# An explicit weight load ahead of two waits in each step of a recurrence on TensorE

## What is computed

```python
x = x + L0(x, cond)          # adaptive low-rank MLP over 4 x 512 rows of 256
x = x + L1(x, cond)          # a recurrence over the 512 time steps:
xW = jnp.einsum('ntd,dh->nth', x, Wx) + b
def step(prev_h, xw_t):
    next_h = jnp.tanh(xw_t + prev_h @ Wh)     # prev_h is 4 x 256, Wh is 256 x 256
    return (next_h, next_h)
```

## Time and profile before

| | us |
|---|---|
| median of 3 runs | 568.93 |
| lowest, highest run | 568.4, 570.08 |
| the profiled execution, its time | 569.51 |
| the profiled execution, its span from first to last instruction | 567.6 |
| of this, from the first tanh of the recurrence (80.49) to the last pair (562.66) | 482.2 |
| TensorE busy with matmuls / with weight loads | 510.9 / 429.1 |
| VectorE / ScalarE busy | 287.8 / 173.9 |

### The profile page before, as it was taken

The page is one execution under the profiler, slowest core; times in us unless marked ns, Lnnn a source line. Parts: engine busy times, 40 slices in busy tenths (PEclk is TensorE's granted clock), DMA queues, the critical chain, the costliest instruction groups (busy, mean ns, idle before and its releaser), DMA issues.

```text
span 567.6 us, 31977 instructions
## 1 busy us (share of the span) xinstructions
PE 510.9 (90%) x14200; PEld 429.1 (76%) x14200; DVE 287.8 (51%) x2214; ACT 173.9 (31%) x1128; POOL 21.6 (4%) x33
## 2 busy tenths in 40 slices
PE   4979989999999999999999999999999999999995
PEld 4334458888888888888888888888888888888884
DVE  2142355555555555555555555555555555555553
ACT  3021113333333333333333333333333333333322
POOL 1039100000000000000000000000000000000000
PEclk9978989999999999999999999999999999999999
DMA  7950000000000000000000000000000000000000
GB/s 259 387 190 0 0 3 4 4 13 5 13 4 13 4 14 4 13 5 10 8 3 14 3 14 3 14 3 14 3 14 3 13 5 14 3 11 6 6 13 12
DMA packets 11216, 15.99 MB, mean 28 GB/s; under 512 B 1587, under 2 KB 6978, under 8 KB 11074
## 3 DMA queue, kind: packets, MB, share of 16 engines
q1 hardware_dynamic: 11078, 13.95, 7.4%
HBM read 11.85 MB, written 2.10 MB: 25 GB/s over the span
## 4 chain that ended last, share of the span: by engine, by line
PE 82%; ACT 8%; issue 3%; SPq 3%; DMA 3%; DVE 0%; DVEq 0%
PE bank L653 66%; ACT w_sb L358 8%; PE bank L633 7%; PE bank L589 3%; DMA w_sb<-in_L_cond_W 3%; PE bank L601 2%; SPq L227 2%; PE bank L642 1%; PE bank L628 1%; PE bank L571 1%; PE bank L578 1%; PE bank L515 0%; PE bank L554 0%; ACT xT L315 0%; DVE x2T L446 0%
## 5 line engine op out<-in xcount | busy, mean ns | idle before, releaser
L653 PE MATMUL bank<-w_sb,whp 128*128 128x52 bf16 x6132 | 244.2, 186 | 38.7 <-ACT w_sb L358 38.0
L653 PEld LDWEIGHTS bank<-w_sb,whp 128*128 128x128 bf16 x6132 | 188.5, 96 | 86.8 <-ACT w_sb L358 64.5
L479 DVE TENSOR_TENSOR r_ring<-w_sb 128x4 f32<-128x4 f32 x1022 | 136.6, 164 | 220.9 <-ACT w_sb L358 218.5
L358 ACT ACTIVATE w_sb<-bank 128x4 f32<-128x4 f32 x1024 | 142.2, 174 | 324.7 <-PE bank L653 324.7
L653 PE MATMUL bank<-r_ring,whp 128*128 128x52 bf16 x4096 | 220.7, 186 | 0.0
L653 PEld LDWEIGHTS bank<-r_ring,whp 128*128 128x128 bf16 x4096 | 174.7, 96 | 0.0
L653 PE MATMUL bank<-l_ring,whp 128*128 128x52 bf16 (+1 forms) x2048 | 157.5, 178 | 0.0
L484 DVE TENSOR_TENSOR l_ring<-r_ring 128x4 bf16<-128x4 f32 x1024 | 135.9, 162 | 0.0
L653 PEld LDWEIGHTS bank<-l_ring,whp 128*128 128x128 bf16 x2048 | 122.3, 96 | 0.0
L633 PE MATMUL bank<-xp,wxp 128*128 128x32 bf16 x1536 | 76.2, 176 | 0.0
L633 PEld LDWEIGHTS bank<-xp,wxp 128*128 128x128 bf16 x1536 | 56.2, 95 | 0.0
(11 more groups left out here) (84 smaller groups left out, 147.6 us busy)
## 6 DMA issues: line engine op xcount, KB each, us to landing
w_sb<-in_L_cond_W SPq DMA_DIRECT2D x8, 1024.0 KB, 14.0
x_sb<-in_x SPq DMA_DIRECT2D x4, 512.0 KB, 9.6
out<-o_sb SPq DMA_DIRECT2D x64, 32.0 KB, 1.6
w_sb<-in_L_cond_W SPq DMA_DIRECT2D x1, 256.0 KB
up_sb<-in_L_cond_base_up SPq DMA_DIRECT2D x1, 256.0 KB, 3.1
down_sb<-in_L_cond_base_down SPq DMA_DIRECT2D x1, 256.0 KB, 11.1
wh_sb<-in_L_cond_Wh SPq DMA_DIRECT2D x1, 256.0 KB
wx_sb<-in_L_cond_Wx SPq DMA_DIRECT2D x1, 256.0 KB
```

The lines of the kernel that those rows point to most:

```text
L358: nc.scalar.activation(h_ring[:, m, slot(pair, s), 0:B], zt, ACT.Tanh).then_inc(h_ready, 1)
L479: nc.vector.tensor_tensor(r_ring[:, k, q, 0:B], state_before(pair, s, k)[:, 0:B], state_hi_before(pair, s, k)[:, 0:B], ALU.subtract).then_ ...
L653: return nc.tensor.matmul(zbank(p, q, m)[:, col0:col0 + n], whp[part][:, k, P * m:P * (m + 1)], rhs[:, 0:n], start=False, stop=stop, skip_ ...
```

## The change

Two calls of `nc.tensor.ldweights` are added in the step, 1024 in the whole program. Each names the block of weights that the first matmul behind the next wait uses: `whp[0][:, 0, 0:P]` for h0 and `whp[0][:, 1, 0:P]` for l1. No wait, no matmul and no other engine's instruction is changed.

```diff
+                    nc.tensor.ldweights(whp[0][:, 0, 0:P])
                     for k in range(K2):
                         pe.wait_ge(h_ready, done + k + 1)
                         for m in range(K2):
...
                     pe.wait_ge(l_ready, done + 1)
                     product(0, 0, 0, l_ring[:, 0, q, :])
+                    nc.tensor.ldweights(whp[0][:, 1, 0:P])
                     pe.wait_ge(l_ready, done + 2)
                     product(0, 1, 0, l_ring[:, 1, q, :], stop=True).then_inc(z_ready, 1)
```

## The result

The changed kernel takes 576.36 us (median of 4 runs, 576.2 to 578.56); beside it the kernel before took 569.1 (568.4 to 570.08). The ratio is 1.0135, with a 95% interval of 1.0106 to 1.0164: slower by about 7 us. The profiled execution has a span of 574.4 us.

The account below looks back on a forecast made before the run. The recurrence was taken as the bound, 512 steps of 0.944 us with two cycles meeting at l1. Nothing at h0 and 1 ns a step at l1 add 0.5 us to 568.93, giving 569.4 us; range 567.0 to 580.0.

Parts of the forecast that it names:

- The bound and its unit: The recurrence's 512 steps of 0.944 us bound the kernel; one nanosecond in a step is 0.51 us.
- Both cycles meeting at l1: The cycle through half 1's l_ring and TensorE's own queue reach l1 within some nanoseconds, the first being later.
- h0's 14 ns: At h0, 198 ns against a 184 minimum; saving it only keeps TensorE's queue from becoming the later cycle.
- The matmul keeps its own load, and the wait stays on it: At h0 and l1 the order is extra load, held load, matmul; 15224 loads, 14200 matmuls, the 14 ns stay.
- The h0 load costs nothing: At h0 the extra load ends by 301.03, ahead of the held load at 301.11; cost nothing.
- The l1 load costs 0 to 3 ns: At l1 the extra load mostly fits into the 20 ns waited anyway; taken as 1 ns a step, +0.5 us.
- The upper row, 96 ns: At l1, the upper bound: a whole load record of 96 ns makes the held load 75 ns late, 38 us.
- Rival 2: At l1 the extra load takes its own slot, perhaps awaiting a matmul; 14 to 25 ns, 576 to 582 us; chance 0.30.
- Rival 1: Only one load remains, ahead of the wait; l1 saves 14 ns a step, 7.2 us, giving 561.8 us; chance 0.14.
- Rival 3: At l1 the second load waits for the matmul in flight to end; 160 ns, 82 us, 651 us; chance 0.05.

Follow-up runs that it names:

- the bare l1: Against the kernel before: an explicit load ahead of l1's wait, and l1's matmul issued without a load of its own; 561.17 us against 567.72, 928 ns a step.
- the kernel with two: Against the kernel before: two extra loads in a row ahead of l1's wait, none at h0; 594.84 us against 568.02, 999 ns a step.

## Why the prediction was right or wrong

**The bound and its unit.** 1 ns of a step is 0.51 us: right. The changed step, 17 ns longer, gives 8.7 us in the recurrence, and the time moved by 7.3, within the few us by which the first part scatters. (The 944 ns of the prediction are the mean with the first steps at the lower clock; at a granted clock of 1.00 the step is 942.) Both cycles meeting at l1 within some 20 ns: right, and shown from both sides. The extra load made TensorE's queue the later one; the bare l1 took 14 ns out of the cycle through VectorE; and only then did h0's 14 ns count, for 4 more in the step.

**The matmul keeps its own load, and the wait stays on it:** right. 15224 loads against 14200 matmuls, h0 and l1 at their old 198 and 178 ns.

**The h0 load costs nothing:** right, 942 ns.

**The l1 load costs 0 to 3 ns:** this step failed, and with it the forecast of 569.4. By the sign that the prediction itself named, a step that moves by over 3 ns, it was wrong: the step moved by 17. I took for the least distance of two loads the 20 ns between l1's held load and the one behind it, and the 25 ns of a pair. Both are distances with a matmul between. Without one it is 40 ns: 302.52 to 302.56, and again in the kernel with two. In the kernel before, l1's load started 48 ns behind the load of half 0's `l_ring` matmul; now the extra load starts 25.9 ns behind that one and l1's 39.6 ns behind the extra one. That is 65.5 against 48.2 ns, and so the price is 17 ns. I had said that the trace has no two bf16 loads without a matmul between them, and gave the missing number the value of its neighbours; the price stood on nothing but that. The upper row, 96 ns, was further off still.

**Rival 2** was the case that came, with 0.30: a slot of the extra load's own at l1, 14 to 25 ns, 576 to 582 us. Its second condition, a distance above 25 ns, is what the trace shows. The mechanisms that it offered fit less well than its price: if weights left their place only by a matmul that takes them up, three loads in a row could not follow each other 40 ns apart with no matmul between them; and the second of these distances, with no new matmul ahead of it to pass, was the same 40 ns as the first. The runs also exclude the same block read twice, the wait, and the columns of the extra load. What sets the 40 ns, and why they become 64 and more at the lower clock, stays open. The range of 567.0 to 580.0 held the time only because it reached into this rival; that was no merit of the forecast, which gave the outcome "slower" 0.39 and "same" 0.47.

**Rival 1's price** was sized well, though it didn't happen in the change: 14 ns a step and 7.2 us were worked out for one load ahead of the wait, and 13 ns a step and 6.6 us (561.17 against 567.72) were measured when l1's own load was left out. The run shows that the 14 ns go with that load (178 to 164 ns); that they are the time in which it shifts in was my reading. That h0's 14 ns would bring nothing was off by 4 ns a step, or 2 us.

**Rival 3**, the wait for the matmul in flight to end, is excluded: 40 ns, not 160. In the changed kernel each extra load at l1 started 1 to 2 ns behind the start of the `l_ring` matmul ahead of it, and the held load 40 ns later, while that matmul still had over 140 of its 184 ns to go.

## What to carry to other kernels

A matmul call brought its own weight load here, also behind an explicit one (15224 loads against 14200 matmuls), so the explicit load ahead of a wait was a second load. At a granted clock of 1.00 it cost 17 ns a step at l1, where the wait left less than 40 ns for it, and nothing at h0, where it left some 180 ns in the step shown above (302.83 to 303.01). The weights came ahead of the wait only when the matmul behind it was issued without its own load, behind an explicit load (928 ns a step) or behind the matmul directly ahead that uses the same block (921 ns). In this recurrence that was worth 13 ns a step at l1, and 18 with h0 as well, where the queue no longer stood in the way. When a price isn't in the trace, a distance measured with another instruction between is no bound for it.

## What the runs showed of the hardware

- Two bf16 weight loads without a matmul between them started 40 ns apart at l1, with 128 columns, with a load of 32 followed by one of 128 (39 ns), with the same and with different weights. With a matmul between them it was 25 ns, and 15 ns behind a held load.
- At the granted clock of 0.5 the same distance was 64 to 67 ns in the first steps of the changed kernel, that of pairs 41 to 45, and that behind a held load still 15. In the kernel with two extra loads the first distance was 65 and 64 ns at that clock, the second 47 and 46.
- With its weight load held by the wait l1 took 14 ns longer (178 against 164 ns), and the matmul behind started 38 ns after it instead of 25; without a load of its own behind the same wait it had 164 and 25. With both waits in front of bare matmuls it also started 53 ns behind the end of VectorE's instruction; in the kernel before the held load and its matmul started 53 and 58 ns behind it.
- A bare matmul whose operands were ready followed a matmul by 25 ns, as a pair does, with 52 columns ahead of it and with 4.
- The part ahead of the recurrence took 77.1 to 80.9 us in these profiles, with the granted clock of its middle at 0.50 to 1.00, in kernels whose code there is the same.
